# adaLN transformer layer on 8 cores: x ahead of half the modulation weights, first head's K and Q gathered in PSUM

## The reference

```python
mod = (_silu(L0_c) @ L0_wmod).reshape(4, 6, 1, -1)     # six vectors of 2048 per sequence
sa, ca, ga, sb, cb, gb = (mod[:, i] for i in range(6))
h = _layernorm(x) * (1 + ca) + sa
x = x + ga * attention(h, W_Q, W_K, W_V, W_O)          # 16 causal heads of 128
h = _layernorm(x) * (1 + cb) + sb
x = x + gb * ffn(h)                                    # top 2 of 8 experts and a shared one
```

## Time and profile before

| what | us |
|---|---|
| median of 3 runs | 2230.4 |
| the three runs | 2208.19, 2230.4, 2237.2 |
| the profiled execution | 2210.06 |
| its span (core 5, the slowest) | 2208.5 |
| spans of the other cores | 2185.4 to 2203.6 |

### The profile page before, as it was taken

One profiled execution on the slowest core, in us unless ns is written; L12 is line 12 of the kernel. 1 busy time (PEld: TensorE's weight loads), 2 busy tenths in 40 slices (PEclk: granted clock), 3 DMA queues, 4 the chain that ended last, 5 costly groups with the idle time before them and its releaser, 6 DMA issues.

```text
span 2208.5 us, 30252 instructions; the slowest of 8 cores (2185.4 to 2208.5 us)
## 1 busy us (share of the span) xinstructions
PE 1895.6 (86%) x11971; PEld 1102.5 (50%) x11971; DVE 772.5 (35%) x1445; ACT 453.9 (21%) x692; POOL 274.4 (12%) x465
## 2 busy tenths in 40 slices
PE   2449899999999999987888799986979779697698
PEld 1225566666666666653344355644536344453243
DVE  3541354454444444445476211110111101010077
ACT  2331323223233223222111101010111101011011
POOL 1110000100000000001001322111203111121021
PEclk9778999999999999997899999998989889899799
DMA  9995234354544434357847679999999999999977
GB/s 215 228 205 92 39 58 77 64 81 71 80 73 75 77 62 64 58 87 141 203 157 153 105 135 185 173 188 182 197 183 181 193 177 186 185 182 186 223 245 251
DMA packets 81361, 315.65 MB, mean 143 GB/s; under 512 B 12352, under 2 KB 12992, under 8 KB 73024
## 3 DMA queue, kind: packets, MB, share of 16 engines
q0 software_dynamic: 63936, 237.31, 63.8%
q1 hardware_dynamic: 17280, 76.34, 9.9%
HBM read 480.89 MB, written 42.60 MB: 237 GB/s over the span
## 4 chain that ended last, share of the span: by engine, by line
PE 68%; DMA 21%; DVE 6%; issue 3%; ACT 2%; POOL 0%; another core or an unknown queue 0%; DVEq 0%; SPq 0%; ACTq 0%; POOLq 0%
DMA rD<-wd 12%; PE pj L595 10%; PE sc L956 10%; PE pj L561 8%; PE sc L1137 7%; PE pj L577 5%; PE pj L1161 5%; DMA rA<-wmod 3%; PE pj L813 3%; PE pj L416 3%; PE pz L735 3%; PE sc L663 3%; PE pz L1161 2%; PE pj L1328 2%; DMA xl<-ximg 2%
## 5 line engine op out<-in xcount | busy, mean ns | idle before, releaser
L1137 PE MATMUL sc<-xgT,rD 128*128 128x320 bf16 x2048 | 282.4, 301 | 1.3 <-DVE xgT L1109 1.3
L561 PE MATMUL pj<-hT,rA 128*128 128x512 bf16 x1024 | 241.0, 386 | 4.9 <-DVE hT L538 2.8
L595 PE MATMUL pj<-wv,hT 128*128 128x256 bf16 x2048 | 244.2, 273 | 0.0
L956 PE MATMUL sc<-h,rD 128*128 128x512 bf16 x1024 | 229.1, 386 | 16.3 <-ACT acts L964 8.3
L1137 PEld LDWEIGHTS sc<-xgT,rD 128*128 128x128 bf16 x2048 | 201.5, 98 | 81.9 <-issue 1.4
L670 DVE TENSOR_REDUCE negm<-sc 128x1 f32<-128x2048 f32 (+7 forms) x128 | 169.3, 1354 | 183.3 <-PE sc L666 177.9
L673 ACT ACTIVATE pb<-sc,negm 128x2048 bf16<-128x2048 f32 (+7 forms) x128 | 155.4, 1217 | 372.7 <-DVE negm L670 154.4
L1161 PE MATMUL pj<-rD,acte 128*128 128x512 bf16 (+1 forms) x512 | 141.3, 414 | 101.8 <-DMA rD<-wd 94.4
L595 PEld LDWEIGHTS pj<-wv,hT 128*128 128x128 bf16 x2048 | 196.9, 98 | 25.9
L956 PEld LDWEIGHTS sc<-h,rD 128*128 128x128 bf16 x1024 | 100.2, 99 | 139.9 <-issue 25.3
L719 DVE COPY pt<-trf 128x1024 bf16<-128x1024 bf16 (+1 forms) x160 | 101.9, 637 | 172.9 <-PE trf L711 172.9
(11 more groups left out here) (131 smaller groups left out, 1999.3 us busy)
## 6 DMA issues: line engine op xcount, KB each, us to landing
rA<-wmod POOLq DMA_DIRECT2D x96, 512.0 KB, 14.3
rD<-wg POOLq DMA_DIRECT2D x64, 512.0 KB, 27.3
rD<-wu POOLq DMA_DIRECT2D x64, 512.0 KB, 24.8
rD<-wd POOLq DMA_DIRECT2D x64, 512.0 KB, 33.7
xl<-ximg SPq DMA_DIRECT2D x16, 1024.0 KB, 11.5
yd<-yp SPq DMA_DIRECT2D x32, 512.0 KB, 11.2
rA<-wk POOLq DMA_DIRECT2D x16, 512.0 KB, 6.2
rA<-wq POOLq DMA_DIRECT2D x16, 512.0 KB, 6.2
```

The costliest lines, as they stand in the source:

```text
L561: tm = P.op(T, lambda t, dc=dc, b=b, q=q: t.matmul(pj[:, b * 512:(b + 1) * 512], buf[:, dc * 128:(dc + 1) * 128], hT[:, dc * 2048 + q * 51 ...
L595: tm = P.op(T, lambda t, dc=dc, b=b, k=k, c0=c0: t.matmul(pj[:, b * 512 + k * 256:b * 512 + (k + 1) * 256], hT[:, c0:c0 + 128], wvb[i][dc ...
L956: tm = P.op(T, lambda t, dc=dc, buf=buf, w=w: t.matmul(sc[:, 1024 + w * 512:1536 + w * 512], buf[:, dc * 128:(dc + 1) * 128], bass.AP(h2, ...
L1137: tm = P.op(T, lambda t, dc=dc, buf=buf, w=w: t.matmul(sc[:, 1024 + w * 512:1024 + w * 512 + CAP], buf[:, dc * 128:(dc + 1) * 128], xT[:, ...
```

## The change

The x loop keeps four of the eight modulation numbers (0, 4, 1, 5, at steps 5, 9, 13 and 17). The other four come behind it. The weights of head 0 for K and Q are loaded first of all on GpSimd's queue behind the constants, into two of the later probability buffers (`pb[2]`, `pb[3]`). K and Q of head 0 are no longer built by `gen_K` and `gen_Q`. Six PSUM banks (the four of `sc`, `trf`, `pz`) stay open over all feature blocks: for each group g of four feature blocks the hidden blocks are scaled and 24 matmuls added to the six sums. Groups 0 and 1 follow on the x loop; ahead of groups 2 and 3 stand their modulation numbers. At the end ScalarE copies the six banks out.

```diff
+    s_kq0 = [DSem(P, f"s_kq0_{i}") for i in range(2)]
+    kq0_ld = [P.dma(G, pb[2 + i][:, :], (d_wk, d_wq)[i][0, :, :], s_kq0[i]) for i in range(2)]
     for j in order:
         ring.want(mod_srcs(j))
...
-        if i >= 2 and i % 2 == 1 and i // 2 - 1 < 8:
-            run_all(gen_mod(order[i // 2 - 1], ring))
+        if i in (5, 9, 13, 17):
+            run_all(gen_mod(order[(i - 5) // 4], ring))
...
-    for dc in range(DC):
-        hT_mod.append(P.op(V, lambda v, dc=dc: v.tensor_scalar(
-            hT[:, dc * 2048:(dc + 1) * 2048], hT[:, dc * 2048:(dc + 1) * 2048],
-            modc[:, 16 + dc:17 + dc], modc[:, dc:dc + 1], ALU.mult, ALU.add),
-            [mod_done[dc // 4], mod_done[4 + dc // 4], hT_v, hT_s]))
+    kq_ps = [sc[:, q * 512:(q + 1) * 512] for q in range(4)] + [trf[:, :], pz[:, :]]
+    kq_tok = {}
+    def modulate(g):
+        for dc in range(4 * g, 4 * g + 4):
+            hT_mod.append(P.op(V, lambda v, dc=dc: v.tensor_scalar(
+                hT[:, dc * 2048:(dc + 1) * 2048], hT[:, dc * 2048:(dc + 1) * 2048],
+                modc[:, 16 + dc:17 + dc], modc[:, dc:dc + 1], ALU.mult, ALU.add),
+                [mod_done[g], mod_done[4 + g], hT_v, hT_s]))
+    def kq_group(g):
+        for u in range(6):
+            w = 0 if u < 4 else 1
+            for dc in range(4 * g, 4 * g + 4):
...
+                kq_tok[u] = P.op(T, lambda t, u=u, w=w, dc=dc, mvg=mvg: t.matmul(
+                    kq_ps[u], pb[2 + w][:, dc * 128:(dc + 1) * 128], mvg, start=(dc == 0), stop=(dc == DC - 1)),
+                    [kq0_ld[w], hT_mod[dc]] + ([sc_free[u]] if g == 0 and u < 4 else []), inc=(dc % 4 == 3))
+    for g in range(4):
+        if g >= 2:
+            run_all(gen_mod(g, ring))
+            run_all(gen_mod(4 + g, ring))
+        modulate(g)
+        kq_group(g)
...
+    for u in range(6):
+        if u < 4:
+            kt[0] = sc_free[u] = P.op(S, lambda s, u=u: s.activation(
+                kb[0][:, u * 512:(u + 1) * 512], kq_ps[u], AF.Copy), [kq_tok[u]])
+        else:
+            qt[0] = P.op(S, lambda s, u=u: s.activation(
+                qb[0][:, (u - 4) * 512:(u - 3) * 512], kq_ps[u], AF.Copy, scale=SCALE), [kq_tok[u]])
...
-    ring.want([d_wk[0, :, :], d_wq[0, :, :]])
...
-    run_all(gen_K(0))
-    run_all(gen_Q(0))
     run_all(gen_V(0, range(8)))
```

More of the change, by code:

```diff
@@ L529, in build_nc @@
             fr_c(i - 2)
-        if i >= 2 and i % 2 == 1 and i // 2 - 1 < 8:
-            run_all(gen_mod(order[i // 2 - 1], ring))
-    assert len([j for j in order if j in mod_done]) == 8
-    mod_last = max((mod_done[j] for j in order), key=lambda t: t[1])
+        if i in (5, 9, 13, 17):
+            run_all(gen_mod(order[(i - 5) // 4], ring))
     hT_v = [t for t in hT_evs if t[0] is P.sem[V]][-1]
@@ L536, in build_nc @@
     hT_mod = []
-    for dc in range(DC):
-        hT_mod.append(P.op(V, lambda v, dc=dc: v.tensor_scalar(
-            hT[:, dc * 2048:(dc + 1) * 2048], hT[:, dc * 2048:(dc + 1) * 2048],
-            modc[:, 16 + dc:17 + dc], modc[:, dc:dc + 1], ALU.mult, ALU.add),
-            [mod_done[dc // 4], mod_done[4 + dc // 4], hT_v, hT_s]))
+    kq_ps = [sc[:, q * 512:(q + 1) * 512] for q in range(4)] + [trf[:, :], pz[:, :]]
[10 more added lines that the diff above has]
+            for dc in range(4 * g, 4 * g + 4):
+                if w == 0:
+                    mvg = hT[:, dc * 2048 + u * 512:dc * 2048 + (u + 1) * 512]
+                else:
+                    mvg = bass.AP(hT, dc * 2048 + (u - 4) * 1024, [[DC * 2048, 128], [256, 4], [1, 128]])
+                kq_tok[u] = P.op(T, lambda t, u=u, w=w, dc=dc, mvg=mvg: t.matmul(
[7 more added lines that the diff above has]
+        kq_group(g)
     kt, qt, vtk = {}, {}, {}
@@ L564, in gen_K @@
                     start=(dc == 0), stop=(dc == DC - 1)),
-                    [ld, pj_free[b], hT_mod[dc]] if dc == 0 or h == 0 else (), inc=(dc == DC - 1))
+                    [ld, pj_free[b]] if dc == 0 else (), inc=(dc == DC - 1))
                 yield 1.0
@@ L640, in slot_gens @@
             yield from gen_mod(j, ring, ga_b if j < 12 else gb_b)
-    pb_free = {(i, k): t_tab0 if i == 0 else None for i in range(4) for k in (False, True)}
+    pb_free = {(i, k): t_tab0 if i == 0 else kq_tok[5] for i in range(4) for k in (False, True)}
     pt_free = [None] * 3
     pt_rot = [0]
-    tr_free = [None]
-    pz_free = [None, None]
+    tr_free = [qt[0]]
+    pz_free = [qt[0], qt[0]]
     col_free = [None] * 8
```

## The result

The changed kernel is **slower by 0.65%**: 2236.8 us in the median of 20 runs against 2228.8 for 20 runs of before, ratio 1.0065 with an interval of 1.0040 to 1.0089. I had forecast slower by 1.4%, 2262.3 us, range 2226 to 2282. The direction and the range hold, the size doesn't: 14 us by the ratio, against 31.9. The difference is smaller than the 2% that the prediction counts as no change; the interval is clear of 1 all the same.

What follows compares the result with a forecast made beforehand. The prediction took DMA to bound the opening stage and TensorE the rest from V(0): V(0) 29.4 us later plus 2.5 for half clock, +31.9, on the median 2230.4 gives 2262.3 us, range 2226 to 2282.

Steps and rivals of the forecast that it cites:

- the row of 5.2: x loop: profile row giving 5.2 us for a lone x load, which the prediction used for its quick blocks.
- The 4.4 us: x loop: the skill page's estimate for a 1 MB load; by it three quick blocks would save about 2 us.
- The bound from the volume: Before V(0): two more units, 6.2 us, put its weights at 191.8 even with DMA never idle; gain at most 3.4 us.
- the last line of the sum: Whole kernel: +31.9 us added to the median of the runs shown, 2230.4, rather than the profiled 2210.1, giving 2262.3.
- the term +31.9: Start of V(0): 29.4 us later (224.6 against 195.2) plus 2.5 us for its half-clock start.
- From V on, all as before: Behind V(0)'s start: nothing changes, so the whole +31.9 us reaches the end.
- My walk: Opening stage: queues followed through x loop, turn and tail, x15 landing at 132.4, V(0) at 224.6; case +26 to +37, chance 0.55.
- A: Opening stage: DMA never runs dry, V(0) between 191.8 and 195.2, up to 3.4 us faster; with up to +10, chance 0.05.
- B: x loop and turn: x15 at 120 to 126 or shorter waits, +10 to +26 us; chance 0.20 together with D.
- C: Groups 0 and 1 stay at half clock, to 170.9, and x gains nothing: +37 to +48 us; chance 0.20.
- D: V(0) doesn't wait for its weights: V(0) at 214 at best, +19 us; chance 0.20 together with B.
- The step on groups 0 and 1: Behind the x loop: their 48 matmuls ahead of number 2 hold its buffers, leaving the DMA idle 7.7 us.

Runs made afterwards that it cites:

- e7: Changed kernel with five x buffers, modulation numbers 2, 6 and 3 between gathering groups, V(0)'s weights right behind the last modulation unit; ratio to before 0.9962.
- e9: e7 with modulation number 5 at step 16 of the x loop instead of 17, and number 7 in the middle of gathering group 2; ratio to before 0.9938.
- the first control: The kernel before, run again unchanged; V(0) came at 192.7 to 196.5 us, and the end 2012.4 us after the latest V(0).
- the order alone: Kernel before with only the new modulation order (four numbers in the x loop, four behind it), K and Q built as before; ratio 1.0121.
- the dose (c2): Kernel before with 140 added matmuls (30.2 us of TensorE, no DMA) ahead of V(0), second run; ratio to before 1.0143.
- e2: Changed kernel with the loads of V(0)'s weights moved from behind the ring's units to the end of the x loop; ratio to before 1.0042.
- e8: Changed kernel with modulation number 2 between gathering groups 0 and 1 instead of behind both; ratio to before 1.0111.
- the gathering alone: Changed kernel with all eight modulation numbers back at their old x loop steps and the four gathering groups following each other; ratio to before 0.9987.

## Why the prediction was right or wrong

**Right: what bounds the stage and where the price arises.** The DMA bounds it, V(0) sets the rest, and everything that counts is the idle time of the DMA engines. Step by step on the latest core, forecast and measured: x9 at 83.7 and 84.4, x15's landing 132.4 and 132.8, number 5's first release 145.1 and 145.4, the release behind groups 0 and 1 165.4 and 166.3, the last modulation unit 199.9 and 202, end of the gathering 214.1 and 215.0, V(0) 224.6 and 225.9, released by the weights' DMA. V(0) then took 1.3 us longer for its start at the low clock on cores 3 and 4 and 2.2 to 2.6 on the other six, where I had 2.5; the length of the wait doesn't order them. The first scores came 31.7 us later, my sum was 31.9. Two quick loads of x took 4.9 and 5.4 us from issue to landing on core 3 (issued near 79 and 84), as the row of 5.2 said. The 4.4 us from the Trainium skill ("DMA: Bandwidth & Descriptors", section "Anatomy of one DMA"), which the prediction set beside it, were too little, and the page gives its fit for loads issued by GpSimd's queue, while x comes by SyncE's. The bound from the volume, that no order of TensorE's work brings V(0) below 191.8 with the queue as it stands, was not broken by any kernel that kept that queue; e7 and e9 are below it because they take six units out from in front of V's weights.

**Wrong: the last line of the sum.** "The forecast is for a median: 2230.4 + 31.9 = **2262.3**." The price was read off an execution in which every core had a mean granted clock of 0.929 or more (2210.1 us), and I put it on a median 20 us above that execution without asking what made the two differ. It was the clock of some cores, as far as the record goes: beside the first control every execution of before above 2220 had a core at 0.921 or less. That is no property to which the price adds. The change's median, 2236.8, lies where its executions with all clocks up lie, while in the twenty of before that it was compared with only 4 fall within 2204.7 to 2217.3; their clocks are not on record, so that part is read from their times. On the profiled execution's own base the forecast was 2242.0, against 2237.0 in the profile. I had both bases on the page and chose by the metric's name.

**Mis-sized: the term +31.9 itself, carried from the first scores to the end.** The prediction says "From V on, all as before". With clocks up the kernels lie 26 us apart, the profiled spans 26.9, the two ratios say 23 and 14; none says 31.9. In the profiles the step that lost 5 us can be named: the core that ended last before (core 5) needed 1985.3 us from its first scores to its end, the one that ended last after (core 3) needed 1980.3, and 32.0 - 5.0 is 27.0. The latest core at V(0) is not the core that needed longest behind it. Nor did each core repeat its own time: core 3 needed 1973.0 before and 1980.3 after, core 5 went from 1985.3 to 1961.7. Why is open.

In the mean of the cores the move was smaller from the start: first scores +27.4 (250.2 against 222.7), spans +22.5 (2219.2 against 2196.7). My walk gives one V for all, 224.6; the mean over the cores was 220.0, and x15 landed at 125.0 to 132.8, 128.2 in the mean, against my 132.4. Nothing in the walk picks the latest core, so that it met that one so closely is in part luck. Behind the first scores the mean is 1974.0 for before and 1972.5 in its second profile, 1969.0 and 1971.0 for the change, 1968.6 for the order alone, 1976.9 for the dose (c2) and 1978.1 for e9. Some 1.5 to 5 us may be given back where the cores come to V(0) apart, but e9's cores are 7 us apart and it has the longest time, so this isn't shown; a run that spreads the cores without any other change wasn't made.

**The rivals.** A (DMA never dry) is out, B (a fuller loop) describes some cores, those with x15 at 125, and not the one that counted. C's clock didn't come: groups 0 and 1 ended at 164.75, not 170.9. D was priced right: e2, where V's weights are there, has V(0) at 215.8, the rival said 214. The step on groups 0 and 1 was right as a description of the hole and wrong as advice: e8 closed it and opened three others.

## What to carry to other kernels

Where DMA bounds a stage, sum its idle time, and follow the queue to the last transfer that the next stage waits for: whatever prefetch stands in front of that transfer is part of the path. A load order that looks better ("x first") is only as good as the number of its buffers; at the start of V(0) five instead of three were worth 22 us here, and the order with three cost 30. And when the profiled execution and the median differ by as much as the effect, find out what made them differ before adding an effect read in the one to the other.

## What the runs showed of the hardware that I had not expected

A core's granted clock can stay between its two levels. In the profile of the gathering alone, core 0 has, in stages of its heads:

```profile
300.00:400.00 100.00, 99.29 (x563) 57.01 (x570) 41.02 (x67) 25.20 (x42) 7.39 (x14) 0.81 0.44 70
...
800.00:900.00 100.00, 97.20 (x731) 65.58 (x740) 46.33 (x79) 29.27 (x50) 7.40 (x14) 1.00 0.41 68
```

TensorE is full in both, but the mix of shapes differs, so one shape is the fairer measure: V's matmuls of 128x256 (line 617) took 305 ns in the first stage and 273 in the second. Stages down to 0.2 us within the first say 0.81 too, so it isn't a mean of two levels, and all stages from 250 to 740 us say it. Cores 2 and 3 stood at 1.00 in both stages. The first matmul of the output projection came at 1129.7 on this core and at 1037.8 on core 2.

The cores of a pair (0 and 1, 2 and 3, and so on) part in the kernels in which the x loop leaves the DMA idle for part of its time: x15's statistics start at 127.0 and 129.8, 125.0 and 132.8, 131.4 and 125.2, 125.4 and 129.2 in the change, from 139.2 to 141.6 before. With five x buffers, where the share is 1.01 to 1.03 up to 120 us, they start from 107.8 to 111.2. Which of the two is ahead changes from one execution to the next (core 1 is late in the first profile, core 0 in the second).
